# A transformer layer on one core: another order of the same steps (V projection, transposes of u, PV and FFN steps) on every engine

## What is computed

```
qkv = x @ Wqkv + bqkv                        # 16 heads of 16 features
scores = q . k * 1/16                        # blocks of 128 positions, each sees itself
mask: |kpos - qpos| <= 128                   # and its two neighbour blocks
out = softmax(scores) @ v
x = layernorm(x + out @ Wout + bout)
Wq1, Wq2 = ternary(W1), ternary(W2)          # clip(round(W / (mean|W| + 1e-5)), -1, 1)
h = relu(x @ Wq1.T + b1)                     # 1024 hidden features
x = layernorm(x + h @ Wq2.T + b2)
```

## Time and profile before

| | before |
|---|---|
| median of 3 runs | 1227.82 us (1227.03 to 1229.11) |
| the profiled execution | 1229.44 us, its span 1227.7 us |
| busy, share of the span | PE 88%, PE weight loads 65%, DVE 70%, ACT 50%, POOL 42% |
| granted TensorE clock, mean | 0.927 of full |
| DMA | 80.5 MB, 66 GB/s |
| one row in steady state | 71.66 us |

### The profile page before, as it was taken

The page is one execution under the profiler, slowest core; times in us unless marked ns, Lnnn a source line. Parts: engine busy times, 40 slices in busy tenths (PEclk is TensorE's granted clock), DMA queues, the critical chain, the costliest instruction groups (busy, mean ns, idle before and its releaser), DMA issues.

```text
span 1227.7 us, 28104 instructions
## 1 busy us (share of the span) xinstructions
PE 1074.5 (88%) x8132; PEld 794.1 (65%) x8132; DVE 861.3 (70%) x2934; ACT 611.0 (50%) x1258; POOL 520.0 (42%) x824
## 2 busy tenths in 40 slices
PE   4778998989898899989899998998999899897956
PEld 3445666767666676766667676666767666675746
DVE  2977768777776777777677777768777776777433
ACT  4255545545454554555455454545545454554521
POOL 2233453435445343544534354453435445344430
PEclk8688899998989999898989989899998989899988
DMA  6644424444342444434244443424444342442000
GB/s 173 94 70 71 71 39 86 70 78 64 66 69 40 79 71 78 65 65 69 41 73 76 78 63 66 69 35 81 74 78 62 67 69 35 62 79 37 19 18 18
DMA packets 56924, 80.51 MB, mean 66 GB/s; under 512 B 7729, under 2 KB 27697, under 8 KB 56882
## 3 DMA queue, kind: packets, MB, share of 16 engines
q1 hardware_dynamic: 56882, 80.00, 38.5%
HBM read 20.19 MB, written 8.39 MB: 23 GB/s over the span
## 4 chain that ended last, share of the span: by engine, by line
PE 69%; DVE 10%; issue 7%; ACT 4%; DMA 3%; POOL 3%; SPq 2%; DVEq 1%; POOLq 1%; ACTq 0%
PE shared L517 11%; PE shared L609 11%; PE shared L498 11%; PE st_a L473 11%; PE shared L596 10%; PE st_b L473 4%; PE shared L592 3%; DMA k_stack<-qk_lo 3%; DVE mx L830 3%; PE shared L527 2%; PE shared L578 2%; DVE x L922 2%; PE mx L489 2%; POOL ln_rstd L1036 1%; SPq L388 1%
## 5 line engine op out<-in xcount | busy, mean ns | idle before, releaser
L830 DVE CUSTOM_DVE_ANT_0 mx<-mx,band 128x384 f32<-128x384 f32 (+1 forms) x1024 | 480.8, 512 | 218.7 <-PE mx L489 215.4
L684 ACT ACTIVATE probs<-st_a 128x384 f32<-128x384 f32 (+1 forms) x384 | 202.1, 526 | 357.6 <-PE st_a L473 355.4
L489 PE MATMUL mx<-k_stack,q_stack 48*128 48x384 f32 (+1 forms) x1024 | 280.9, 373 | 14.1 <-DVE rmax L830 11.5
L997 POOL TENSOR_SCALAR_AFFINE_SELECT probs<-probs 128x512 f32<-128x512 f32 (+1 forms) x256 | 129.8, 531 | 333.6 <-ACT probs L684 333.4
L684 ACT ACTIVATE probs<-st_b 128x384 f32<-128x384 f32 (+1 forms) x384 | 201.1, 524 | 0.2 <-PE st_b L473 0.2
L473 PE MATMUL st_a<-q_stack,k_stack 50*128 50x384 f32 (+1 forms) x512 | 185.1, 402 | 4.3 <-ACT probs L684 3.5
L489 PEld LDWEIGHTS mx<-k_stack,q_stack 48*128 48x128 f32 x1024 | 168.9, 199 | 22.7 <-DVE rmax L830 19.7
L517 PE MATMUL shared<-probs,v_aug 128*32 128x384 f32 (+1 forms) x2048 | 154.0, 442 | 0.9 <-issue 0.9
L609 PE MATMUL shared<-w2q,hid_hi 128*128 128x256 f32 x512 | 133.6, 295 | 20.8 <-DVE hid_lo L915 20.8
L596 PE MATMUL shared<-x1T_hi,w1q 128*128 128x256 f32 x512 | 151.2, 310 | 0.0
L596 PE MATMUL shared<-x1T_lo,w1q 128*128 128x256 f32 x512 | 147.8, 306 | 0.0
(11 more groups left out here) (107 smaller groups left out, 1955.7 us busy)
## 6 DMA issues: line engine op xcount, KB each, us to landing
q_stack<-qk_hi SPq DMA_DIRECT2D x128, 128.0 KB, 4.3
k_stack<-qk_hi SPq DMA_DIRECT2D x128, 128.0 KB, 5.3
x_raw<-in_xT SPq DMA_DIRECT2D x16, 512.0 KB, 5.1
q_stack<-qk_lo SPq DMA_DIRECT2D x64, 128.0 KB, 3.9
k_stack<-qk_lo SPq DMA_DIRECT2D x64, 128.0 KB, 5.4
y<-in_x SPq DMA_DIRECT2D x16, 512.0 KB, 5.9
out<-x SPq DMA_DIRECT2D x32, 256.0 KB, 2.1
probs<-in_w2T SPq DMA_DIRECT2D x1, 1024.0 KB, 10.5
```

Source lines behind the costliest of these rows:

```text
L489: mm = pe.matmul(PMX[i % N_MAX][:, col:col + n], SQ[rows, hd, W * m:W * m + W], SK[rows, hd, k0:k0 + n], start=True, stop=True)
L684: act.activation(PR[:, v % 2, g // 2, lo:lo + n], PST[i % 2][:, 0:n], ACT.Exp, scale=SCALE) \
L830: mx = dve.tensor_tensor_reduce(ps, ps, band, 1.0, -3e38, ALU.add, ALU.max, RMAX[:, g, m:m + 1])
L997: pool.affine_select(out=pr_before, in_=pr_before, compare_op=ALU.is_ge, fill=0.0, base=0, pattern=[[0, n], [1, W]], channel_multiplier=-1)
```

## The change

The steps of all four quads are put in another order, and `COST` of the PV halves rises from 1300 to 2200, which moves the groups of units. The second half of the V projection goes from quad 1 to quad 0, qk 2 from quad 0 to quad 1. In quad 0 the first V half stands between `pvb` and `ut`, the second between `ut` and the transposes of `o_norm`. In quad 1 `ut` stands before the transposes of x1 instead of behind them, and qk 3 behind them instead of before. In quad 2 `nmt` moves one FFN step ahead. In quad 3 the PV step stands between the last `f1` and `f2`, and `ut` behind `f2`. On POOL the test that starts the fourth copy to `v_aug` moves with it; POOL's and SP's instructions keep their order.

```
 SIDE = [
-    [("qk", 0), "nmt", "pva", "pvb", "ut", ("vp", 0), ("ot", 0), ("ot", 1), ("qk", 1), ("qk", 2), ("op", 0),
+    [("qk", 0), "nmt", "pva", "pvb", ("vp", 0), "ut", ("vp", 1), ("ot", 0), ("ot", 1), ("qk", 1), ("op", 0),
      ("op", 1)],
-    [("ln1", 0), ("ln1", 1), ("ln1", 2), ("vp", 1), "nmt", ("ln1", 3), "pva", "pvb", ("x1", 0), ("x1", 1),
-     ("x1", 2), ("x1", 3), ("qk", 3), ("x1t", 0), ("x1t", 1), "ut", ("f1", 0, 0)],
-    [("f1", 0, 1), ("xs", 0), ("f1", 0, 2), ("f1", 0, 3), ("xs", 1), "nmt", "pva", "pvb", ("f2", 0), "ut",
+    [("ln1", 0), ("ln1", 1), ("ln1", 2), ("qk", 2), "nmt", ("ln1", 3), "pva", "pvb", ("x1", 0), ("x1", 1),
+     ("x1", 2), ("x1", 3), "ut", ("x1t", 0), ("x1t", 1), ("qk", 3), ("f1", 0, 0)],
+    [("f1", 0, 1), ("xs", 0), "nmt", ("f1", 0, 2), ("xs", 1), ("f1", 0, 3), "pva", "pvb", ("f2", 0), "ut",
      ("f1", 1, 0)],
-    [("f1", 1, 1), "nmt", "xr", ("ln2", 0), ("ln2", 1), ("f1", 1, 2), "pva", "pvb", ("f1", 1, 3), "ut", ("f2", 1),
-     ("ln2", 2), ("ln2", 3)],
+    [("f1", 1, 1), "nmt", "xr", ("ln2", 0), ("ln2", 1), ("f1", 1, 2), ("f1", 1, 3), "pva", "pvb",
+     ("f2", 1), "ut", ("ln2", 2), ("ln2", 3)],
 ]
...
-        "nmt": (256, 1), "f1": (2560, 10), "f2": (8192, 32), "pva": (1300, 1), "pvb": (1300, 1)}
+        "nmt": (256, 1), "f1": (2560, 10), "f2": (8192, 32), "pva": (2200, 1), "pvb": (2200, 1)}
...
-                            if v == 0 and step == "ut":
+                            if v == 0 and step == "pvb":
                                 v_in_place(b, 3, at == 0)
```

## The result

The change makes the kernel faster: 1192.73 us median of 4 runs (1190.05 to 1195.88) against 1228.14 us for the kernel before on the same chip, a ratio of 0.971, 95% interval 0.968 to 0.974. The profiled execution took 1195.88 us, its span is 1194.1 us. Medians in this document are of all runs of a kernel, ratios and intervals of those within 1.5% of its fastest run.

What follows compares the result with a forecast made beforehand. PE was taken as nearest to full, a row being its work at the granted clock plus its waits. Terms summed to -1.35 us a row, -19 us over fourteen rows and 1 us at the ends: 1208 us, range 1197 to 1232.

Steps and rivals of the forecast that it cites:

- quad 0, wait that stays: Quad 0, before the V projection, the next user of bank 0 after qk 0: PE still waits 0.4 us.
- quad 0, new wait before the output projection: Quad 0: one qk step instead of two covers the evacuation of the o_norm transposes, so PE waits 0.7 us.
- the stretch from there to x1: Quad 1: the x1 chain on DVE starts earlier, taken as -0.4 us a row.
- m4 to the x1 transposes: Quad 1: from reduction m4, behind which DVE starts the x1 chain, to PE's x1 transposes; unchanged at 5.24 us.
- the term +1.0: Quad 1: qk 3 now stands behind the x1 transposes instead of `ut`, adding 1.0 us a row.
- The ends: The bodies at both ends of the run: 1 us more gained, beside fourteen rows with all parts.
- Quad 0's first gain: Quad 0: reduction m2 moves into the PV step, so the wait for DVE's qk_lo shrinks by 1.15 us.
- The clock rival: Low stretch in quad 1 grows to 10.2 us, another follows the wait before qk 0 every second row: 1244 us, chance 0.13.
- DVE and the copies of quad 3: Two rivals: DVE bounds quad 1, 1224 us, chance 0.14; late copies hold quad 1's max units, 1225 us, chance 0.05.
- Theory A: Experiments' theory: what PE does around the x1 transposes decides how long the clock stays low.
- B: Experiments' theory: the moment a row's wait meets the clock's own changes decides; row length carries it to the next row.

Runs made afterwards that it cites:

- quad 3 alone: Kernel before with only quad 3's new order (PV step between the last f1 and f2, `ut` behind f2): 1231.08 us, ratio 1.000.
- the old `COST`: Changed kernel with the costs of the PV halves back at 1300: 1282.55 us, ratio 1.040.
- its repeat: Changed kernel measured once more, unaltered, against the kernel before on the same chip: 1189.69 us, ratio 0.968.
- quad 0 alone: Kernel before with the new quad 0, and qk 2 in place of the V half in quad 1, costs as before: 1252.16 us, ratio 1.017.
- quad 1 alone: Kernel before with only qk 3 and `ut` of quad 1 exchanged around the x1 transposes: 1246.40 us, ratio 1.013.
- put back: Changed kernel with qk 3 of quad 1 again ahead of the x1 transposes and `ut` behind them: 1226.44 us, ratio 0.997.
- both runs on `COST`: PV halves' costs back at 1300 in the changed kernel, 1282.55 us (1.040); raised to 2200 alone in the kernel before, 1248.84 us (1.013).
- the other bank: Changed kernel with `ut` of quad 3 on the bank of that quad's PV step: 1186.27 us, ratio 0.965.
- the eight matmuls: Eight more matmuls a row in the second half of f1: changed kernel 1219.62 us (0.990), kernel before 1240.31 us (1.009).
- the version whose steady rows have no low stretch: Changed kernel with qk 2 of quad 1 moved ahead of `ut` and quad 3's `ut` on its PV step's bank: 1139.81 us, ratio 0.927.

## Why the prediction was wrong

The direction was right, and so were nearly all of its waits; the size was wrong by 15 us. The table gives single steps; below it the row is added up by stretches.

| step of the prediction | forecast | measured |
|---|---|---|
| quad 0, wait that stays | 0.4 us | 0.33 us |
| `ut` of quad 0 | no wait | no wait |
| quad 0, new wait before the output projection | 0.7 us | 0.64 us |
| the stretch from there to x1 | -0.4 us | -0.6 us |
| quad 1, wait of `ut` | 1.2 us | 1.41 us |
| quad 1, wait for x1 | 2.2 us | 1.79 us |
| m4 to the x1 transposes | 5.24 us | 5.24 us |
| before the second f2 | no wait | no wait |
| last f2 matmul to qk 0 | about 2 us | 1.9 us |
| low stretch behind x1, lost (count) | 3.4 us | 1.7 us |
| a row | 70.3 us | 68.24 us |

| stretch of a row, mean of eleven rows | before | after | forecast change | measured change |
|---|---|---|---|---|
| x1 transposes to `ut` of quad 2 | 21.81 us | 20.97 us | +1.0 us | -0.8 us |
| `ut` of quad 2 to the second f2 | 13.04 us | 10.99 us | -1.9 us | -2.05 us |
| last f2 matmul to qk 0 | 1.23 us | 1.92 us | +0.8 us | +0.7 us |
| qk 0 to the x1 transposes | 30.26 us | 28.96 us | -1.25 us | -1.3 us |

- **The step that failed** is the sentence "The sum leaves the low stretch behind x1 at 3.4 us lost." It was 1.7 us, by count, in every steady row of the profiled execution. Of the 2.1 us between forecast and measured row, 1.8 lie in the stretch behind the x1 transposes, where the term +1.0 (qk 3 for `ut`) was added with the low stretch left as it was. The other 0.3 lie in terms that were each off by 0.05 to 0.15. The runs put the price of a stretch of 6.8 us over one of 3.4 at 1.4 us by duration and 1.7 by count, so the clock is nearly all of it, and the term +1.0 may have been 0.1 to 0.4 too high. The case was seen (a row of 0.6 us less and 1199 us, with a chance of 0.05), but too small a size and too small a chance were put on it, and the range ended above the result.
- **The ends were mis-sized too.** The prediction had them 1 us faster. They are 7.1 and 3.5 us slower. What the clock takes by count, one minus its mean times the length, is 0.17 x 137.02 = 23 us before and 0.22 x 144.16 = 32 us after at the beginning, and 17 and 23 us at the end. So by this count the clock takes all of the loss there. In the whole run it takes 0.073 x 1227.7 = 90 us before and 0.066 x 1194.1 = 79 us after. Of the 33.6 us of the span, 11 are thus the clock's, and 23 everything else, against 20 in the sum. The thirteen rows in the middle gave back 24 us of clock by this count, and the ends cost more than half of it.
- **Quad 0's first gain** was right in size (1.2 us of wait less), but it belongs to `COST`: with the old number the wait is 1.54 us again. The prediction booked the new number for this alone; with the old one the kernel is 78 us slower or more, most of it by low stretches and waits elsewhere.
- **The clock rival** had its mechanism right and its kernel wrong. The low stretch behind the wait before qk 0 appears with quad 3 alone and with the old `COST`, and in the changed kernel once, in its repeat. A stretch of 10.2 us around x1 appears in eight of the variants (quad 0 alone, quad 1 alone and put back, both runs on `COST`, the other bank, the eight matmuls in both kernels), and in no steady row of the changed kernel.
- **The Trainium skill** (TensorE: Matmul & The Clock Gate, A second HAM failure mode: psum-queue depth-cycling) has frequent short idles between groups of matmuls send the clock back and forth. The runs agree for 1.33 us before qk 0 in one kernel; 1.22 us at the same place in the changed kernel did it once in the steady rows of two executions. Both kernels have five waits over 0.25 us a row, and the time at the lower level halved, so the number of waits doesn't set it.
- **DVE and the copies of quad 3** did not become bounds. ACT's wait for `k_stack` (16.9 us in eleven waits before) is gone, as forecast, and the chain from m4 did not start later.

Theory A falls with the other bank, with the eight matmuls and with the repeat. B is what is left, and the repeat and the falls 71.68 us apart speak for it, but it is a description: the length of the stretch depends on when in the clock's own changes the wait falls, and the kernel can settle in one state. It gave no time in advance for most variants. What exactly makes the chip lower its clock is open, and so is why the beginning of the changed kernel sits lower. No run was made that shifts the wait alone, by a known amount, with all else in place; that would be the direct test of B.

## What to carry to other kernels

When a profile shows the clock falling behind one wait that comes in every iteration, price the wait with its low stretch (here 2.1 us, and for 6.8 us at the lower level 2.1 more by duration or 3.4 by count), and take it away altogether. A change that only moves or shortens the wait may give or take 1.7 us an iteration for reasons that its own instructions don't show, and its range must hold that. If the steady iterations are a whole number of the shortest low stretch long, expect the clock to take back small gains. And try the parts of a reordering together: here each part tried costs or gives nothing alone, because one edit creates the wait that another covers.

## What was not expected of the hardware

- The low stretches in steady rows have few lengths: 3.4, 6.8 or 10.2 us (once 13.7, in quad 1 alone), in all the kernels here, whatever stands inside them; at the ends of a run they are up to 30.7 us long (the other bank). By count they cost 1.7, 3.4 or 5.1 us; measured by duration in the changed kernel's order, 0.65 us for the first 3.4 and 1.4 for the next.
- In the changed kernel and its repeat the fall comes up to 2.7 us ahead of the transposes or 0.4 to 0.7 us behind their start; in the kernel before 0.5 to 1.8 us behind it, each 71.68 us after that of the row before. It can come ahead of the transposes, so a part of it can lie in the wait itself.
- An execution can settle: rows of 68.27 us with the fall always at the same point, after several rows in which it moved about. The same kernel therefore spreads over 1185 to 1199 us, where the version whose steady rows have no low stretch stays within 1139.17 to 1140.54.
- Eight matmuls of 0.12 us in another quad (13 us in a run) cost 20 to 27 us in one kernel, and 12 in the other.
